# Feed-forward weights turned in 32x32 squares by VectorE during the attention, and two chunks of the first tile's gate and up products placed around the last output projection

## What is computed

```python
x = x + attention(layernorm(x), ctx, ctx)                  # x: 16 x 224 x 512, ctx: 16 x 750 x 512, 16 heads of 32
n = quant(layernorm(x))                                    # 16 x 224 rows = 28 tiles of 128 rows
h = silu(n @ quant(w_gate).T) * (n @ quant(w_up).T)        # w_gate, w_up: 1408 x 512
x = x + quant(h) @ quant(w_down).T                         # w_down: 512 x 1408
# quant: in blocks of 16 along the last axis, scale = max|x| / 6, values rounded to the grid 0, .5, 1, 1.5, 2, 3, 4, 6
```

## Time and profile before

| | us |
|---|---|
| median of 3 runs (2173.25 to 2178.88) | 2176.15 |
| the profiled execution, whole | 2174.35 |
| its span, first to last instruction | 2172.5 |
| PE busy | 2090.3 (96%) |
| DVE busy | 1681.3 (77%) |
| ACT busy | 863.0 (40%) |

### The profile page before, as it was taken

The page is one execution under the profiler, slowest core; times in us unless marked ns, Lnnn a source line. Parts: engine busy times, 40 slices in busy tenths (PEclk is TensorE's granted clock), DMA queues, the critical chain, the costliest instruction groups (busy, mean ns, idle before and its releaser), DMA issues. The chain is left out here.

```text
span 2172.5 us, 42294 instructions
## 1 busy us (share of the span) xinstructions
PE 2090.3 (96%) x16862; PEld 1799.9 (83%) x16862; DVE 1681.3 (77%) x2811; ACT 863.0 (40%) x1753; POOL 144.1 (7%) x162
## 2 busy tenths in 40 slices
PE   6999999999999999999999999978999999999998
PEld 5888888888888888889888888857787887887786
DVE  5677777777777776777777777867898988998985
ACT  5555455455554554545445555442111111111111
POOL 0000000000000000000000000001110001000100
PEclk9999999999999999999999999999999999999999
DMA  4443444534444445344453453443433443334331
GB/s 158 117 123 94 126 105 121 137 95 118 129 100 123 106 122 138 91 115 105 123 131 96 118 139 90 115 137 114 115 112 102 127 118 107 107 122 123 107 111 42
DMA packets 144675, 248.69 MB, mean 114 GB/s; under 512 B 31984, under 2 KB 89328, under 8 KB 142048
## 3 DMA queue, kind: packets, MB, share of 16 engines
q1 hardware_dynamic: 143760, 244.68, 41.5%
q10 hardware_dynamic: 720, 1.31, 0.2%
HBM read 101.23 MB, written 48.89 MB: 69 GB/s over the span
## 5 line engine op out<-in xcount | busy, mean ns | idle before, releaser
L730 DVE TENSOR_REDUCE row_max<-max_bank 128x1 f32<-128x376 f32 (+1 forms) x896 | 450.4, 537 | 162.4 <-PE max_bank L552 161.5
L631 ACT ACTIVATE probs<-score_bank 125x448 f32<-125x448 f32 x768 | 399.7, 541 | 290.5 <-PE score_bank L566 287.6
L526 PE MATMUL proj_bank<-attention_operands 128*128 128x256 f32 x2304 | 304.7, 282 | 0.0
L566 PE MATMUL score_bank<-qstack,kstack 103*128 103x224 f32 x1536 | 300.0, 282 | 1.4 <-DMA kstack<-k_low 1.3
L504 PE MATMUL proj_bank<-attention_operands 128*128 128x376 f32 (+1 forms) x1536 | 292.0, 339 | 8.3 <-DVE k_low L752 4.8
L526 PEld LDWEIGHTS proj_bank<-attention_operands 128*128 128x128 f32 x2304 | 288.9, 189 | 0.1
L566 PEld LDWEIGHTS score_bank<-qstack,kstack 103*128 103x128 f32 x1536 | 256.0, 191 | 37.0 <-issue 35.1
L504 PEld LDWEIGHTS proj_bank<-attention_operands 128*128 128x128 f32 x1536 | 264.6, 191 | 11.9 <-DVE k_low L752 6.4
L1339 ACT ACTIVATE f_act_gate<-gate_bank 128x512 f32<-128x512 f32 (+1 forms) x84 | 47.2, 562 | 554.4 <-PE up_bank L1279 554.4
L1279 PE MATMUL gate_bank<-gate_up,early 128*128 128x512 f32 (+1 forms) x1008 | 234.1, 382 | 23.9 <-DVE f_hidden L1435 22.0
L1279 PEld LDWEIGHTS gate_bank<-gate_up,early 128*128 128x128 f32 x1008 | 186.2, 191 | 63.5 <-issue 32.3
(11 more groups left out here) (135 smaller groups left out, 2678.4 us busy)
## 6 DMA issues: line engine op xcount, KB each, us to landing
kstack<-k_low SPq DMA_DIRECT2D x256, 93.8 KB, 2.4
kstack<-early SPq DMA_DIRECT2D x256, 93.8 KB, 2.2
kstack<-k_high SPq DMA_DIRECT2D x256, 93.8 KB, 2.2
strips_scratch<-f_strips SPq DMA_DIRECT2D x25, 960.0 KB, 3.7
f_turned<-strips_scratch SPq DMA_DIRECT2D x100, 240.0 KB, 4.4
ctx_raw<-in_ctx SPq DMA_DIRECT2D x15, 1500.0 KB, 7.6
qstack<-early SPq DMA_DIRECT2D x384, 28.0 KB, 1.9
qstack<-q_part SPq DMA_DIRECT2D x384, 28.0 KB, 1.8
```

The lines of the kernel that those rows point to most:

```text
L526: last = nc.tensor.matmul(out[:, 0:256], ctx_part[cs][:, c, kt * KW:kt * KW + P], w_hi_lo[W_V][ws][:, c, half * 256:(half + 1) * 256], sta ...
L566: last = nc.tensor.matmul(score_bank[j % 2][:, k * SQ:(k + 1) * SQ], kstack[t % 2][0:STK, j, kt * KW:kt * KW + P], qstack[t % 2][:, j, :], ...
L631: nc.scalar.activation(probs[p][:, j, :, :], score_bank[j % 2][0:KW, 0:2 * SQ].rearrange("p (k q) -> p k q", k=2), ACT.Exp, scale=float(DK ...
L730: nc.vector.tensor_reduce(row_max[:, m, kh:kh + 1], mbank[:, 0:KSPLIT[kh + 1] - KSPLIT[kh]], AX.X, ALU.max).then_inc(max_reduced, 1)
```

## The change

- `ffn_square`: after the ninth step of a share, DVE transposes it in 32x32 squares (128x352) into `fw_square`. `ffn_store` stores that to a new tensor `ffn_squares`. `ffn_load` now waits for a transpose instead of a store.
- `ffn_regroup` (place 6.0 of the slot after): where a share completes a tile of 512 columns, SP issues four transfers from HBM to HBM, 32x4x128 each, that put the squares in place. 33 tiles give 132 such transfers.
- The host lays out the weights so that the squares come out as the matmuls need them. The products `turn` and `down_turn` of PE are gone. ACT and DVE make the high and low parts from `turn_raw` in SBUF.
- `turn_raw` has four buffers instead of three. 16 tiles of gate and up are split in slots 2 and 3 of the last batch, 8 in each, 4 ahead of the last output projection and 2 between its halves.
- `first_gate`: chunk 0 of tile 0's gate and up products ahead of the last output projection, chunk 1 behind it, in front of the barrier. The feed-forward part then begins with chunk 2 of tile 0.
- `period_units`: `hidden` of chunk 0 moves forward in periods 0 to 2; x is loaded one period earlier (`load` of tile n+4 in period n, behind `load_res`) instead of at the head.
- The eleven down tiles: 5 in period 0, 6 in period 1, with four buffers (`late_turn`, `late_turn_lo`).

```diff
-RAWS = 3
+RAWS = 4
...
+        add(at["ffn_quant"][-1] + 0.02, ("ffn_square", m))
...
+            add(6.0, ("ffn_regroup", m if slot + 1 < NG else m - 3))
...
-    for j in range(len(GATE_UP)):
-        g, at = (2, 1.5 + 1.02 * j) if j < 10 else (3, 0.3 + 0.93 * (j - 10))
-        placed.append((g, at, ("turn", j)))
+    for j in range(SLOT_TILES):
+        g, at = (2, 1.5 + 1.25 * j) if j < 8 else (3, 0.3 + 1.3 * (j - 8))
         placed.append((g, at + 0.35, ("turn_hi", j)))
         placed.append((g, at + 0.7, ("turn_lo", j)))
-        if j + RAWS < len(GATE_UP):
-            placed.append((g, at + 0.4, ("turn_load" if j > 4 else "turn_load_early", j + RAWS)))
+        if j + RAWS < EARLY_TILES:
+            placed.append((g, at + 1.4, ("turn_load" if j > 4 else "turn_load_early", j + RAWS)))
...
-END_UNITS += [("ffn_store", 2), ("inverse", 3, 0), ("inverse", 3, 1), ("heads", 3), ("heads_hi", 3), ("sum_lo", 3), ("out", 0, 0), ("out", 0, 1)]
-END_UNITS += [("store_x1", 0, 0), ("store_x1", 0, 1)]
...
+END_UNITS += [("ffn_store", 2), ("inverse", 3, 0), ("inverse", 3, 1), ("heads", 3), ("heads_hi", 3), ("sum_lo", 3), *end_tiles(16, 20), ("first_gate", 0), ("out", 0, 0), *end_tiles(20, 22), ("out", 0, 1)]
+END_UNITS += [("store_x1", 0, 0), ("store_x1", 0, 1), ("first_gate", 1), ("ffn_regroup", 2)]
...
-    turn_raw = [sb(f"turn_raw{r}", [P, D]) for r in range(RAWS)]
+    turn_raw = [sb(f"turn_raw{r}", [P, D]) for r in range(RAWS - 1)]
     in_ctx_raw = ctx_raw[:, :, :].rearrange("p c s -> p (c s)")
     first_work = [[idle[:, n * D:(n + 1) * D] for n in range(3)] for idle in (in_ctx_raw, in_values)]
+    turn_raw.append(in_ctx_raw[:, KC * SK - D:KC * SK])
...
-        if kind == "turn":
-            engine.wait_ge(turn_lo, unit[1] + 1)
-            return
...
-                elif kind == "turn":
-                    pe.wait_ge(turn_loaded[t % RAWS], 16 * (t // RAWS) + 16)
-                    for c in range(KC):
-                        last = nc.tensor.transpose(out[:, c * P:(c + 1) * P], turn_raw[t % RAWS][:, c * P:(c + 1) * P],
-                                                   ident[:, :])
-                    last.then_inc(turned, 1)
+                elif kind == "first_gate":
+                    pe.wait_ge(fs["x_lo"], 1)
+                    pe.wait_ge(turn_lo, 8 * (t + 1))
+                    if t == 0:
+                        pe.wait_ge(max_reduced, 2 * MT * NG * batches)
+                        pe.wait_ge(shift_copied, NG * batches)
+                    else:
+                        pe.wait_ge(exp_done, 12 * NG * batches)
+                    for m in range(2):
+                        n = 0
+                        for c in range(KC):
+                            for xs_, ws in PASSES:
+                                last = nc.tensor.matmul(first_banks[2 * t + m][:, :], xqt[0][xs_][:, c, :],
+                                                        gate_up[m][ws][:, c, CH[t]:CH[t + 1]], start=(n == 0), stop=(n == 11))
+                                n += 1
+                    last.then_inc(fs["gated"], 1)
...
                     n, i = GATE_UP[t]
-                    act.wait_ge(turned, t + 1)
-                    nc.scalar.activation(gate_up[n][0][:, :, i * P:(i + 1) * P],
-                                         where[("turn", t)][:, :].rearrange("p (c k) -> p c k", c=KC),
-                                         ACT.Copy).then_inc(turn_hi, 1)
+                    act.wait_ge(turn_loaded[t % RAWS], 16 * (t // RAWS) + 16)
+                    if t == 0:
+                        act.wait_ge(made["k"], 2 * NG * batches)
+                        act.wait_ge(made["q"], NG * batches)
+                        act.wait_ge(made["v"], 2 * KT * batches)
+                    nc.scalar.activation(in_quarters(gate_up[n][0][:, :, i * P:(i + 1) * P]),
+                                         by_quarter(turn_raw[t % RAWS][:, :]), ACT.Copy).then_inc(turn_hi, 1)
...
+                elif kind == "ffn_square":
+                    chain = 3 * b + t
+                    dve.wait_ge(fw_steps, QSTEPS * (chain + 1))
+                    if chain > 0:
+                        dve.wait_ge(fw_stored[(chain - 1) % 2], 16 * ((chain - 1) // 2) + 16)
+                    nc.vector.transpose(fw_square[:, :], fw_share[chain % 2][:, :]).then_inc(fw_squared, 1)
...
-                    nc.vector.tensor_tensor(gate_up[n][1][:, :, i * P:(i + 1) * P],
-                                            where[("turn", t)][:, :].rearrange("p (c k) -> p c k", c=KC),
-                                            gate_up[n][0][:, :, i * P:(i + 1) * P].bitcast(F32),
+                    nc.vector.tensor_tensor(in_quarters(gate_up[n][1][:, :, i * P:(i + 1) * P]),
+                                            by_quarter(turn_raw[t % RAWS][:, :]),
+                                            in_quarters(gate_up[n][0][:, :, i * P:(i + 1) * P]).bitcast(F32),
...
-            return weights[m].rearrange("r c -> (r c)").rearrange("(p b k) -> b p k", p=P, k=share)[
-                bass.ds(b, 1), :, :].rearrange("b p k -> (b p) k")
+            return weights[m][:, b * share:(b + 1) * share]
...
-                    reached(sp, fw_stored[chain % 2], 16 * (chain // 2))
+                    reached(sp, fw_squared, chain - 1)
                     sp.dma_start(fw_share[chain % 2][:, :], share_of(ffn_raw, chain // batches, chain % batches))\
                         .then_inc(fw_loaded[chain % 2], 16)
                 elif kind == "ffn_store":
                     chain = 3 * b + t
-                    sp.wait_ge(fw_steps, QSTEPS * (chain + 1))
-                    sp.dma_start(share_of(ffn_quant, chain // batches, chain % batches), fw_share[chain % 2][:, :])\
+                    sp.wait_ge(fw_squared, chain + 1)
+                    sp.dma_start(share_of(ffn_squares, chain // batches, chain % batches), fw_square[:, :])\
                         .then_inc(fw_stored[chain % 2], 16)
+                elif kind == "ffn_regroup":
+                    chain = 3 * b + t
+                    n, s = chain // batches, chain % batches
+                    i = FC * s // batches
+                    if FC * (s + 1) // batches > i:
+                        sp.wait_ge(fw_stored[chain % 2], 16 * (chain // 2) + 16)
+                        reached(sp, fw_stored[(chain - 1) % 2], 16 * ((chain - 1) // 2) + 16)
+                        for q in range(HG):
+                            sp.dma_start(
+                                ffn_quant[n].rearrange("(q i) (m g k) -> m q i g k", q=HG, m=FC, g=HG)[i, q, :, :, :],
+                                ffn_squares[n].rearrange("(g i) (m q k) -> m q i g k", g=HG, m=FC, q=HG)[i, q, :, :, :])\
+                                .then_inc(regrouped[n], 16)
...
-    spread = has(-1) or has(2)
-    return [*when(3, ("load", n + 3)), *when(0, ("gate_up", n, 0)), *quant(1, 2, 3, 4, 5, 6), *when(3, ("norm", n + 3)),
-            *quant(7), *when(-3, ("store", n - 3)), *when(-1, ("load_res", n - 1)), *when(-2, ("h_hi", n - 2)),
-            *when(1, ("x_hi", n + 1)), *quant(8), *when(0, ("hidden", n, 0)), *when(3, ("normalize", n + 3)), *quant(9),
-            *when(-2, ("h_lo", n - 2)), *when(0, ("gate_up", n, 1), ("hidden", n, 1), ("gate_up", n, 2)),
-            *([("strips", n, has(-1), has(2))] if spread else []), *when(1, ("x_lo", n + 1)),
+    hidden_at = {0: 0, 1: 6, 2: 6}.get(first, 8)
+
+    def quant_and_hidden(*steps):
+        return [u for s in steps for u in quant(s) + (when(0, ("hidden", n, 0)) if s == hidden_at else [])]
+
+    return [*when(0, ("gate_up", n, 0)),
+            *(when(0, ("hidden", n, 0), ("gate_up", n, 1), ("hidden", n, 1)) if hidden_at == 0 else []),
+            *quant_and_hidden(1, 2, 3, 4, 5, 6), *when(3, ("norm", n + 3)),
+            *quant_and_hidden(7), *when(-3, ("store", n - 3)), *when(-1, ("load_res", n - 1)), *when(4, ("load", n + 4)),
+            *when(-2, ("h_hi", n - 2)), *when(1, ("x_hi", n + 1)), *quant_and_hidden(8),
+            *when(3, ("normalize", n + 3)), *quant(9),
+            *when(-2, ("h_lo", n - 2)), *(when(0, ("gate_up", n, 1), ("hidden", n, 1)) if hidden_at else []), *when(0, ("gate_up", n, 2)),
+            *([("strips", n, has(-1), has(2))] if has(-1) or has(2) else []), *when(1, ("x_lo", n + 1)),
             *when(-2, *[("down", n - 2, c) for c in range(3)]), *when(0, ("hidden", n, 2)),
```

159 lines of the change are left out of this document (91 added, 68 removed).

## The result

| | before | after |
|---|---|---|
| median, us | 2174.70 (4 runs) | 2137.56 (2137.12 to 2138.56, 4 runs) |
| span of the profiled execution, us | 2172.5 | 2135.3 |

The ratio is 0.9831, with a 95% interval of 0.9817 to 0.9845: 37 us faster.

What follows compares the result with a forecast made beforehand. TensorE was taken as the bound in the attention, with waits in the last batch and, for x and hidden, in the steady feed-forward part. Terms of -23.3, -9.6, +3.8, -4.8 and +4 sum to -29.9: 2146 us, range 2133 to 2164.

Steps and rivals of the forecast that it cites:

- Term 1: Steady feed-forward, tiles 3 to 25: the wait for x goes and PE's 23.07 us period becomes the bound, -23.3 us.
- Term 3: Last pv to feed-forward block: PE products replace idle time, chunk 0 covers the o_part wait and the clock's fall, +3.8 us.
- Term 2: Last batch up to the last pv: PE loses 22 groups of turn and one long stall, -9.6 us.
- slot 3's first score comes at 1437.35 - 3.1: Last batch: the 3.06 us load stall goes, so this score comes at 1434.3 us.
- Term 4: Feed-forward block's start to tile 3: VectorE's chain stays, hidden comes earlier, +66.3 us instead of 71.1, so -4.8 us.
- Term 5: Attention: the 48 squares on VectorE cost +1 us and the regroup transfers +3, together +4 us.
- Net -0.3 to +1.5 us a batch: Attention, batches 1 to 10: the low stack's change from ctx starting 1.5 us earlier against the regroup's 1.25 to 3.0 us.
- the threshold of 2.7: Attention: the first 2.7 us of a VectorE wait on the low stack cost PE nothing.
- The last batch gains little: Rival, 8%: loads of the 16 tiles on SP behind stacks limit slots 2 and 3, 2152 us.
- The attention is disturbed: Rival, 20%: each regroup costs 1.5 us more than its place gives back, squares push row maxima, 2156 to 2166 us.
- The squares are on the path: Rival in the attention, part of the 20% one: VectorE's square transposes delay the kernel by 24 us, 2166 us.
- Slower, the regroup as a queue: Rival, 3%: the regroup's 512 rows of small pieces delay the low stack in batches 1 to 10, 2182 us or more.

Runs made afterwards that it cites:

- e6: The kernel before with one move, x loaded a period earlier, behind load_res: 2150.18 us, ratio 0.9873 to the kernel before.
- e8: The changed kernel with chunk 0 of tile 0 also behind the last output projection: 2145.19 us, ratio 0.9860 to the kernel before.
- e7: The changed kernel with ScalarE's five weight loads in slot 2 of the last batch put behind the next high part: 2137.91 us, ratio 0.9816.
- e10: The changed kernel with hidden of chunk 0 of tiles 1 and 2 back behind step 8 of the quantization: 2137.24 us, ratio 0.9821.
- e4: The changed kernel with every square transpose on VectorE made twice: 2145.01 us, ratio 0.9850 to the kernel before.
- e3: The changed kernel with every regroup transfer issued a second time, into a spare HBM tensor: 2158.82 us, ratio 0.9913 to the kernel before.
- e1: The changed kernel with the load of a share waiting again for a store, ahead of ctx: 2148.57 us, ratio 0.9866 to the kernel before.
- e5: The kernel before with the next share's load in slot 0 moved behind the loads of ctx and x: 2169.95 us, ratio 0.9963.
- e9: The changed kernel with hidden of chunks 0 and 1 made ahead of norm of tile 2 at the feed-forward block's start: 2140.67 us, ratio 0.9835.

## Why the prediction was right, and where it was wrong

**Term 1 (-23.3, measured -23.25): right for its reason.** The period without the wait was read from one pair of rows of the kernel before, and it came out to the hundredth. e6 shows that it is a part of its own.

**Term 3 (+3.8, measured +3.57): right in sum, and one of its reasons is not borne out.** The 24 + 24 products and the output projection take their 17.5 us in ten executions. The granted clock is 1.00 from 1440 to 1464, so chunk 0 stands there with no fall of the clock behind it. That it is chunk 0 which "covers the fall of the clock" is not shown: without it, in the profiled execution of e8, the clock didn't fall either.

**Term 2 (-9.6, measured -4.96): mechanism right in slot 3, wrong in slot 2.** The step that failed is "slot 3's first score comes at 1437.35 - 3.1". Counted from the first transpose of xn, that score came at 111.3 us before and 111.8 now: the 3.06 us stall went and as much came back, beside 0.55 for the square that stands ahead of slot 2 (forecast 0.6). Slot 2 itself takes 27.04 us in both kernels. The step subtracted the stall and held the rest of slot 2 fixed. ScalarE has less to do there than before (8 high parts and not 10 beside the 12 probabilities); what changed is the order: a load that it issues waited for PE's `turn` before and waits for VectorE's low part now, 0.70 us at a time, with the next probabilities behind it, and PE has no `turn` between the scores. So PE waits where it didn't before, 5.4 us in all for the probabilities and once for `neg_max`:

```profile
1414.91 0.77 PE L579 MATMUL score_bank<-qstack,kstack 103*128 103x224 f32 x2 [1.00 <-ACT probs L654]
...
1419.24 0.77 PE L579 MATMUL score_bank<-qstack,kstack 103*128 103x224 f32 x2 [1.59 <-ACT probs L654]
...
1421.84 0.45 PE L569 MATMUL gate_bank<-ident,neg_max 128*128 128x128 f32 x1 [1.82 <-DVE neg_max L761]
```

And the clock is down for longer: 0.50 for 17 us in slot 2 (from 1409.4), where it was 7 before (from 1428.9). PE is busy 11.5 us of these 17 and 6.2 of the 7, so the lower clock takes some 2.6 us more than before (an estimate, half of the difference). With 1.2 us more of idle time that is about what the ten groups of `turn` had taken. e7 bears it out: the probabilities cost 3.5 us, the clock is down for 10 us, and slot 2 takes 24.9. Slot 3 took 22.7 us before and 17.2 now, -5.5 of a forecast -6.5. What begins the long stretch at half clock wasn't taken apart.

**Term 4 (-4.8, measured -2.1): two sizes off.** `x_lo` of tile 2 came at +39.9 (39.1 forecast) and the down product of tile 0 at +59.7. The forecast's +66.3 for tile 3, less 7.7 for the 33 down products, has it at +58.6, so VectorE's chain through it is 1.1 us late: the 2.4 us for `hidden` were no gain (e10). The other 1.65 us are the clock: the first products ran at half clock behind the 2.76 us wait, 9.35 us from there to tile 3. The 69.0 varies by that, 67.6 to 69.1 in seven executions of the same code.

**Term 5 (+4, measured -10.4 in the profiled execution, some -7 on average): wrong in sign.** Three things stand in it.
- 2.1 us of the 10.4 lie in batch 0 and are within what executions differ by. Batch 0 takes 87.2 to 89.4 us in the eight executions whose attention is that of the changed kernel, with a wait of PE for `row_max` of 2.4 to 3.6 us in it, and 89.5 before. These eight executions reach the last batch at 1317.8 us on average (1314.9 to 1321.1), the two like before at 1325.0.
- The failed step is "Net -0.3 to +1.5 us a batch", and with it "adding -0.3 to +1.5 to ten such waits gives PE -1.5 to +15": measured, the net is -1.46. PE already lost time to these waits, 4.8 us of waits in seven batches (one of them) by which these batches are 8.3 us longer, 1.8 of that from a clock that fell behind one of them. That is what an earlier ctx could give back. The sum had the mechanism (1.5 us earlier) and the threshold of 2.7, and only counted what would come on top.
- The regroup's own cost was set at 1.25 to 3.0 us of the queue. In batches 1 to 10 VectorE's mean wait went from 2.45 to 0.99 us, by all of the 1.5 that ctx gained, so this first copy cost nothing that can be seen. The stack is issued later, but lies behind ctx in any case. The forecast's own test says the same: in batches 11 to 14, with no regroup in that place, the mean wait should be equal or shorter, and it is 1.90, the longer of the two (2.89 before, so it shrank by 1.0 and not by 1.5).

The trap that the Trainium skill names in "VectorE: DVE Perf Modes", section "The three transpose paths", did not show, and these copies, which keep runs of 128 values, don't test it: the regroup's transfers land in 2.8 us at the median from 60 to 1000 us (4.5 in the batch from 490 to 575), not in tens. The same page of the Trainium skill, section "Rules for kernel authors", advises TensorE for a 128x128 transpose whose result may go to PSUM. That would have kept PE's 22 groups here. No run here separates that choice from the rest, but it bears on little of the gain: of the 37 us 23 are a load moved, and some 7 a wait that no longer stands ahead of a large transfer.

**The rivals.** None came whole. "The last batch gains little" came half (5 us of 9.6), with ScalarE's order and the clock in slot 2, and not SP's loads. "The attention is disturbed" had 20% and was on the wrong side. "The squares are on the path" holds in part for a second set (e4). "Slower, the regroup as a queue" needs what e3 shows at its beginning, with another wait than the one it named.

## What to carry to other kernels

Look at what stands ahead of a large transfer on the issuing queue: here a wait of 1.5 us for a store that ctx didn't need cost some 8 us (e1), and they could be had by a move of one unit (e5). When a wait is about to change, count first what it costs today, with the slower clock behind it, as the lower end of the range. When work is taken off an engine in a stretch that waits, ask what it will wait for next: PE's `turn` products went, and slot 2 kept its 27.04 us. And a load that is used each period should be issued a period ahead where its buffer allows it: the time of the free period, read where the loads have ended, tells the gain in advance.

## What was not expected of the hardware

- A stall of PE can cost about twice its length. Waits for `k_low` of 1.82, 1.88 and 2.19 us (e1, before, e9) were followed by a granted clock of 0.50, and made their batches 1.7 to 1.8 us longer than the wait itself. Those of 0.2 to 1.63 us, in all executions but e3 and e4, made theirs longer by at most half a microsecond beyond the wait. Length alone doesn't decide: in e3 a wait of 1.26 us for `row_max` was followed by the lower clock, and so were 3.3 us idle ahead of the output projection in before, e5 and e6, but 3.55 us in e8 were not.
- The same instructions took 67.6 to 69.1 us from the block's start to tile 3, while tiles 3 to 25 agreed within 0.04 us over eleven. In the profiled executions the spread comes from the stretches with idle time.
- Four regroup transfers of 64 KB take 2.6 us to issue on SP. In the batch from 490 to 575 us ctx landed 7.4 us after its issue with them behind it, and 6.6 before, far less than their own 4.5 from issue to landing.
